# An eight-core transformer layer: transposes moved from TensorE to transposing DMAs, and the start loaded in another order

## The reference, cut to what matters

```python
# x: (8, 4096, 1024) f32, 16 heads of 64, causal
def attn(x):
    q, k, v = split(x @ c_attn_kernel.T + c_attn_bias, 3)      # heads of 64
    s = (q / sqrt(64)) @ k.T + causal_bias
    return (softmax(s) @ v).reshape(b, s, 1024) @ c_proj_kernel.T + c_proj_bias
def ffn(x):
    return gelu(x @ w1 + b1, approximate=False) @ w2 + b2       # 1024 -> 4096 -> 1024
x = _layernorm(x + attn(x))
x = _layernorm(x + ffn(x))
```

## Time and profile before

| | us |
|---|---|
| time before, median of 3 runs | 2211.36 (2210.08 to 2312.66) |
| profiled execution, its own time | 2209.44 |
| its span on the slowest core, core 1 | 2207.9 |
| spans of the eight cores | 2200.8 to 2207.9 |
| TensorE busy on core 1 | 2059.6 |
| ScalarE busy on core 1 | 1328.7 |
| VectorE busy on core 1 | 743.2 |

### The profile page before, as it was taken

One profiled execution on the slowest core, in us unless ns is written; L12 is line 12 of the kernel. 1 busy time (PEld: TensorE's weight loads), 2 busy tenths in 40 slices (PEclk: granted clock), 3 DMA queues, 4 the chain that ended last, 5 costly groups with the idle time before them and its releaser, 6 DMA issues.

```text
span 2207.9 us, 65222 instructions; the slowest of 8 cores (2200.8 to 2207.9 us)
## 1 busy us (share of the span) xinstructions
PE 2059.6 (93%) x30380; PEld 1299.5 (59%) x30380; DVE 743.2 (34%) x1925; ACT 1328.7 (60%) x1602; POOL 219.2 (10%) x182
## 2 busy tenths in 40 slices
PE   7999998989999999997788999999999999999997
PEld 3455565555565556654445666666666666666665
DVE  3543334344343443435121322333223223332321
ACT  1799999999999999998995222222222222222222
POOL 2000000000000000001011221222111112221100
PEclk8999999999999999999899999999999999999999
DMA  9500100021000000002954201111110011111000
GB/s 144 81 12 8 36 8 12 19 34 35 8 13 19 8 24 8 12 10 66 169 88 89 51 27 48 49 49 49 48 48 20 30 48 48 48 48 49 20 20 20
DMA packets 53184, 89.73 MB, mean 41 GB/s; under 512 B 3248, under 2 KB 36656, under 8 KB 51888
## 3 DMA queue, kind: packets, MB, share of 16 engines
q0 software_dynamic: 17184, 33.56, 10.0%
q1 hardware_dynamic: 35728, 52.00, 7.1%
HBM read 93.94 MB, written 25.17 MB: 54 GB/s over the span
## 4 chain that ended last, share of the span: by engine, by line
PE 61%; ACT 29%; DVE 7%; DMA 1%; issue 1%; POOL 0%; POOLq 0%; SPq 0%; DVEq 0%; ACTq 0%
ACT work L610 29%; PE ps L1010 20%; PE ps L1028 19%; PE ps L815 5%; PE ps L452 5%; PE ps L665 4%; PE ps L593 4%; DVE qkv L493 2%; DVE work L621 1%; PE ps L284 1%; PE ps L512 1%; DVE work L690 1%; DMA xT<-xb 1%; DVE stat L517 1%; PE ps L858 1%
## 5 line engine op out<-in xcount | busy, mean ns | idle before, releaser
L610 ACT ACTIVATE work<-ps,cb 128x1024 bf16<-128x1024 f32 (+1 forms) x1088 | 1083.8, 1123 | 66.6 <-PE ps L593 61.6
L1018 ACT ACTIVATE work<-ps,b_s 128x256 bf16<-128x256 f32 x512 | 242.3, 473 | 764.1 <-PE ps L1010 764.1
L665 PEld LDWEIGHTS ps<-qkv,work 64*128 64x128 bf16 x16896 | 434.6, 95 | 292.7 <-PE ps L665 82.7
L665 PE MATMUL ps<-qkv,work 64*128 64x65 bf16 x16896 | 569.8, 193 | 17.9 <-DVE work L690 11.6
L1010 PE MATMUL ps<-work,xT 128*128 128x256 bf16 x4096 | 532.2, 273 | 0.4 <-issue 0.4
L1028 PE MATMUL ps<-qkv,work 128*128 128x512 bf16 x1984 | 509.0, 379 | 0.0
L1010 PEld LDWEIGHTS ps<-work,xT 128*128 128x128 bf16 x4096 | 401.3, 98 | 156.2 <-issue 0.5
L593 PE MATMUL ps<-qkv 64*128 64x512 bf16 x2016 | 366.4, 369 | 65.4 <-ACT work L610 57.8
L1028 PEld LDWEIGHTS ps<-qkv,work 128*128 128x128 bf16 x1984 | 192.9, 98 | 164.1 <-ACT work L1018 0.2
L452 PE MATMUL ps<-xT,work 64*128 64x512 bf16 x896 | 258.3, 377 | 2.9 <-DVE stat L517 1.8
L453 PE MATMUL ps<-xT,work 64*128 64x512 bf16 x896 | 258.4, 377 | 0.0
(11 more groups left out here) (74 smaller groups left out, 1262.2 us busy)
## 6 DMA issues: line engine op xcount, KB each, us to landing
work<-x SPq DMA_DIRECT2D x16, 1024.0 KB, 6.3
out<-work SPq DMA_DIRECT2D x15, 1024.0 KB, 4.1
attn_s<-work SPq DMA_DIRECT2D x64, 128.0 KB, 2.0
xT<-w POOLq DMA_DIRECT2D x8, 1024.0 KB, 14.6
work<-attn_s SPq DMA_DIRECT2D x16, 512.0 KB, 7.7
qkv<-w POOLq DMA_DIRECT2D x16, 512.0 KB, 8.3
xT<-xb POOLq DMA_DIRECT2D x7, 1024.0 KB, 45.4
work<-wqk POOLq DMA_DIRECT2D x7, 512.0 KB, 6.1
```

The source lines that it names most:

```text
L610: lambda: sc.activation(pb, ps, AF.Exp, bias=cb[:, 8 * p + g : 8 * p + g + 1], scale=0.125),
L665: r = t.matmul(bank(6 + h)[:, 65 * c : 65 * c + 65], pbuf[i % NP][rows, pc : pc + 128], w[rows, o : o + 65], start=first and j == 0 and c ...
L1018: lambda: sc.activation(hbuf[ui % 4], bank(4 + ui % 2)[:, 0:TB], AF.Gelu, bias=b1[:, hc : hc + 1]),
```

## The change

1. **Turns by DMA.** A new kind of item, `Lane.turn`, is a transposing DMA from SBUF to SBUF. `turn_block` issues one from SP for a block's `attN` (128x512 into `attC`) as soon as the block is divided, with its store behind it. `norm1` issues one from SP for each half of `x2b` (128x1024 into `x2T`) as soon as it is written. The transposes L704 and L858 and the copies L708 and L865 are gone, and `turn_steps` with them. There are 64 of the first kind and 32 of the second, all in SP's one list.
2. **Start.** `wv[0]` is loaded whole, behind all four quarters of group 0. `first_block` computes the values (`go_v`) in one piece of 32 matmuls behind the scores of unit 0 and the sums of squares. The 40 warming matmuls are 26, and 4 more stand behind each quarter of `x`.
3. **x by blocks.** A group of `xT` is one piece of 4096 columns in each partition (`x_col` gives the column).
4. **The table of exp early.** ScalarE computes `exp` of one constant column at the start.
5. **Values of masked units later.** `behind` puts a unit's values in line 4 units behind it for a block's first unit, 3 for a masked one, 2 for the others. Projections may start 6 units behind a pair's start instead of 3, and the loads of `wp` and `w2` are written one block later.

```diff
+    def turn(self, slot, out, in_, *after):
+        slot.value += 16
+        self.items.append(
+            (lambda e=self.eng: e.dma_start_transpose(out, in_), after, (slot.sem, 16))
         )
         return (slot.sem, slot.value)
...
-        first_x.append(pool.dma(
-            slot(f"x0_{f}"), xTv[:, f : f + 2, 0, :],
-            xb_d[0][:, QB * f : QB * f + 2 * QB].rearrange("p (f c) -> p f c", f=2)))
-        if f % 4 == 0:
-            ld_v0.append(pool.dma(slot(f"wv0_{f}"), wv[0][:, 256 * f : 256 * f + 1024],
-                                  wv_d[0][:, 256 * f : 256 * f + 1024]))
-    ld_qk[0], ld_v[0] = ld_qk0[1], ld_v0[1]
+        first_x.append(pool.dma(slot(f"x0_{f}"), xT[:, QB * f : QB * f + 2 * QB],
+                                xb_d[0][:, QB * f : QB * f + 2 * QB]))
+    ld_qk[0] = ld_qk0[1]
+    ld_v[0] = pool.dma(slot("wv0"), wv[0], wv_d[0])
...
-    warm_done = pe.put(warm, t_warm, t_ones)
+    pe.put(lambda: warm(26), t_warm, t_ones)
+    act.put(lambda: sc.activation(lnst[:, 0:1], cexp[:, 0:1], AF.Exp), t_cexp)
...
+    def x_col(a, fc):
+        return 8 * QB * (a // 4) + QB * fc + 128 * (a % 4)
...
             tok = pe.put(lambda fc=fc: go(fc), first_x[fc // 2], ld_qk0[fc // 4], mark=fc == 7)
-            tok_v = pe.put(lambda fc=fc: go_v(fc), ld_v0[fc // 4], mark=fc == 7)
+            if fc % 2 == 1:
+                warm_done = pe.put(lambda: warm(3 if fc < 7 else 4), t_warm, t_ones)
...
         bound(0, 0)
+        tok_v = pe.put(go_v, ld_v[0])
...
-            turns.append((i, p, g))
+            turn_block(p, g)
...
-        def go():
-            r = a = None
-            for c in range(4):
-                r = t.transpose(pb[:, 128 * c : 128 * c + 128], attN[k % 3][:, 128 * c : 128 * c + 128], idb)
-                a = a or r
-            return a, r
-        attN_free[k % 3] = tok = pe.put(go, done, gb_free[u], ld_idb)
-        gb_free[u] = ev = dve.put(lambda: v.tensor_copy(attC[k % 4], pb[:, 0:512]), tok, attC_free[k % 4])
+        attN_free[k % 3] = tok = sp.turn(
+            slot(f"tn{k % 4}"), attC[k % 4].rearrange("p (c q) -> p c q", c=4), attN[k % 3],
+            uev_tok[0], attC_free[k % 4])
         t_attn[p, g] = attC_free[k % 4] = sp.dma(
-            slot(f"at{k % 4}"), attn_d[:, p, QB * g : QB * g + QB], attC[k % 4], ev)
+            slot(f"at{k % 4}"), attn_d[:, p, QB * g : QB * g + QB], attC[k % 4], tok)
...
+        turn(b, c)
+
+    def turn(b, c):
+        x2b_free[c] = t_xT[b, c] = sp.turn(
+            slot(f"tx{b % 2}_{c}"),
+            x2T[b % 2].rearrange("p (f c) -> p f c", f=8)[:, :, 128 * c : 128 * c + 128],
+            x2b[:, 1024 * c : 1024 * c + 1024], t_x2b[b, c], x2T_free.get(b - 2))
...
-            later.append((need, qk_pairs(p, g) + norm_pair(p, g), start_of[p - 1, 0] + 3 if p > 2 else 0))
+            later.append((need, qk_pairs(p, g) + norm_pair(p, g), start_of[p - 1, 0] + 6 if p > 2 else 0))
...
+    def behind(p, g, j):
+        return 4 if j == 0 else 3 if j >= 4 * g else 2
...
-        while turns and i - turns[0][0] >= 5 and not (gb_open[0] and gb_open[1]) and i >= ready[0]:
-            turn_block(*turns.popleft()[1:])
...
-        hold = 3 if units[waiting[0]][2] == 0 and i + 1 < NU else 2
-        while waiting and i - waiting[0] >= hold:
+        while waiting and (i + 1 == NU or i - waiting[0] >= behind(*units[waiting[0]])):
             queue_values(waiting.popleft())
```

More of the change, by code:

```diff
@@ L50, in dma @@
             (lambda e=self.eng: e.dma_start(out=out, in_=in_), after, (slot.sem, 16))
+        )
+        return (slot.sem, slot.value)
+    def turn(self, slot, out, in_, *after):
+        slot.value += 16
+        self.items.append(
+            (lambda e=self.eng: e.dma_start_transpose(out, in_), after, (slot.sem, 16))
         )
@@ L234, in build_nc, with warm @@
     t_warm = dve.put(lambda: v.memset(sq[0], 0.0))
-    def warm():
+    def warm(n):
         a = None
-        for _ in range(40):
+        for _ in range(n):
             r = t.matmul(bank(6), ones, sq[0], start=True, stop=True)
@@ L403, in go @@
                 o = 1024 * qi + 128 * fc
-                r = t.matmul(bank(4 + qi), wqk[0][:, o : o + 128], xT[:, S * fc : S * fc + QB],
+                r = t.matmul(bank(4 + qi), wqk[0][:, o : o + 128], xT[:, QB * fc : QB * fc + QB],
                              start=fc == 0, stop=fc == 7)
@@ L407, in go, with go_v @@
             return a, r
-        def go_v(fc):
+        def go_v():
             r = a = None
             for n in range(4):
-                r = t.matmul(bank(6 + n // 2)[:, 256 * (n % 2) : 256 * (n % 2) + 256],
-                             xT[:, S * fc + 128 * n : S * fc + 128 * n + 128],
-                             wv[0][:, 256 * fc : 256 * fc + 256],
-                             start=fc == 0 and n % 2 == 0, stop=fc == 7, skip_group_check=True)
-                a = a or r
+                for fc in range(8):
+                    r = t.matmul(bank(6 + n // 2)[:, 256 * (n % 2) : 256 * (n % 2) + 256],
+                                 xT[:, x_col(n, fc) : x_col(n, fc) + 128],
+                                 wv[0][:, 256 * fc : 256 * fc + 256],
+                                 start=fc == 0 and n % 2 == 0, stop=fc == 7, skip_group_check=True)
+                    a = a or r
             return a, r
@@ L480, in go @@
                 o1 = 1024 * qi1 + 128 * fc
[L481 removed]
+                xs = slice(8 * QB * g + QB * fc, 8 * QB * g + QB * fc + QB)
                 tok = two_tiles(
@@ L626, in build_nc @@
     t_p = {}
-    turns = deque()
     attN_free = [None] * 3
@@ L679, in put_half @@
             divide(p, g, t_pv[i])
-            turns.append((i, p, g))
+            turn_block(p, g)
     def divide(p, g, tok):
         n = turn_of[p, g] % 3
-        assert all(turn_of[q, h] % 3 != n for _, q, h in turns)
         acc = PS[:, 3072:4096].rearrange("p (h c) -> p h c", h=2)[:, :, 0:260].rearrange(
@@ L840, in norm1 @@
             lambda: gp.tensor_tensor(y, y, b2b, ALU.add), aff, ld_vec["b2"], pool_last[0])
-    def turn_steps(b, early=False):
-        out = []
-        for c in range(2):
-            def go(c=c):
-                if early:
-                    u = gbank()
-                    pb, held = bank(4 + u).bitcast(BF16), gb_free
-                else:
-                    u = pj_next[0]
-                    pj_next[0] = 1 - u
-                    pb, held = bank(6 + u).bitcast(BF16), pj_free
-                def turns():
-                    r = a = None
-                    for f in range(8):
-                        r = t.transpose(pb[:, 128 * f : 128 * f + 128],
-                                        x2b[:, 1024 * c + 128 * f : 1024 * c + 128 * f + 128], idb)
-                        a = a or r
-                    return a, r
-                tok = pe.put(turns, t_x2b[b, c], held[u], ld_idb)
-                x2b_free[c] = tok
-                held[u] = t_xT[b, c] = dve.put(
-                    lambda: v.tensor_copy(
-                        x2T[b % 2].rearrange("p (f c) -> p f c", f=8)[:, :, 128 * c : 128 * c + 128],
-                        pb.rearrange("p (f c) -> p f c", f=8)),
-                    tok, x2T_free.get(b - 2))
-            out.append((2.0, go))
-        return out
+        turn(b, c)
[4 more added lines that the diff above has]
+            x2b[:, 1024 * c : 1024 * c + 1024], t_x2b[b, c], x2T_free.get(b - 2))
     first_block()
@@ L954, in build_nc @@
                 load_w1()
-            if p == NPAIR - 1 and g == 1:
+            if p == NPAIR - 1 and g == 2:
                 load_w2(0, 8, q2_done[NPAIR - 2])
@@ L985, in build_nc @@
             order[1] = True
-    while turns:
-        turn_block(*turns.popleft()[1:])
     end_pe = t_pv[NU - 1]
@@ L1083, in build_nc @@
             extra.extend(rest if b else proj_steps(b + 1))
-        if hc == 20 and b + 1 < NB:
-            extra.extend(turn_steps(b + 1))
         if hc == 2 and b + 2 < NB:
```

26 lines of the change are left out of this document (8 added, 18 removed).

## The result

| | before | after |
|---|---|---|
| time, median of 4 runs, us | 2210.72 | 2230.06 |
| ratio to before, 95% interval | | 1.0096 (1.0079 to 1.0112) |
| first `exp` begins, median of eight cores | 30.0 | 22.9 |
| from there to the first matmul of the second part | 1151.0 | 1188.2 |
| from there to the end of the span | 1022.6 | 1009.4 |

A forecast was written before the change was run, and what follows sets the result against it. TensorE was taken to bound the second part and nearly all of 25 to 100 us, ScalarE's exp the stretch from 100 to 1184 us. Terms -18.3 - 7 - 3 - 4 + 3 = -29.3 gave a 2182 us median, range 2158 to 2204.

The forecast's parts named there:

- The turns have cover ... at 11 us each they still keep up: Attention: attN is reused after 30 us, so turns one at a time keep up with divisions some 10 us apart.
- landing time T: Time for a transposing DMA to land: 4 us for 128x512, 8 us for 128x1024, bounds 2 to 11 us.
- Edits at nothing: Later values, projection starts at +6 units and moved loads of wp and w2 were to cost nothing.
- -18.3 us in the second part: Second part: 240 transposes of 0.076 us each leave a full TensorE, a gain of 18.3 us.
- The rival of late turns: Second part: 128x1024 turns land later than their 28.5 us cover, about 2256 us; chance 0.05.
- -7 us in the attention: From 100 to 1184 us: freed TensorE time shrinks the 34.2 us of exp waiting by a fifth, later values included.
- -3 us before 100 us: Early attention: 2 us from TensorE's transposes removed, 1 us from VectorE copies and the bank freed; 0 to -5 together.
- -4 us at the start: Start: earlier last quarter of x, new order, better clock and faster first matmuls gain 4 us, range 0 to -8.
- +3 us at the end of the attention: Attention's end: block 1's load_at waits behind the last turn, costing 3 us at a 4 us landing, 10 at 11.
- The rival with the other sign: The slower case: second-part turns of 128x1024 take longer than their cover, about 2256 us; chance 0.05.

The follow-up runs named there:

- g3: f2 with only the six attention turns of blocks 55 to 60, beside the loads of w1 and w2, by TensorE, the rest by DMA: 2186.4 us, ratio 0.9897.
- f4: f2 with all 96 turns by DMA: 2219.8 us, ratio 1.0045.
- e3: Changed kernel with the 64 attention turns replaced by plain, non-transposing DMA copies of the same bytes in 256-byte pieces: 2220.0 us, ratio 1.0048.
- e4: Changed kernel with the values' distance as before (3 units for a block's first unit, 2 for others): 2224.0 us, ratio 1.0068.
- e1: Changed kernel with all 64 attention turns back on TensorE: 2216.8 us, ratio 1.0035.
- e2: Changed kernel with only the last nine attention turns back on TensorE: 2204.4 us, ratio 0.9975.
- g1: f4 with each load of w1 and w2 issued only when the one before has landed: 2219.4 us, ratio 1.0045.
- f1: Changed kernel with the values' distance as before and the last nine attention turns on TensorE: 2197.7 us, ratio 0.9946.
- f2: f1 with block 0's projection steps due 44 units ahead instead of 60: 2188.2 us, ratio 0.9900.
- f3: Kernel before with only the 32 turns of x2b by transposing DMA, all else as before: 2203.8 us, ratio 0.9978.
- g2: f2 with all 64 attention turns by TensorE, only those of x2b by DMA: 2192.4 us, ratio 0.9922.

## Why the prediction failed

Forecast 2182 us, range 2158 to 2204; it came to 2230. With three causes taken out (g3, 2186.4) the kernel is where the forecast was, in part by luck: some terms of the sum were too large and others too small. Of the 43.7 us between the two, 33.4 are the six turns (f4 to g3) and 10.2 the values' distance and the projection's due time together (changed kernel to f4). Against before, g3's eight-core medians are -7.1 us to the first `exp`, -3.5 in A and -14.1 in the second part.

1. **"The turns have cover ... at 11 us each they still keep up"** is the step that failed, by 33 us (f4 to g3). I had measured the cover at 51 to 81 us, where DMA is full, and asked only if the landing time T fits. Even there it was close: the first turn, issued at 47.0 us on core 5, took 28.6 us, and the fourth division waited 2.5 us for it. I did not look at the one other stretch in which POOL loads megabytes, 1000 to 1150 us, nor at divisions there. T was to be 2 to 11 us; the 33 turns issued from 1035 to 1128 us on the eight cores took 13 to 31 us, 23 in the median, and the longest in this stretch followed one another without a pause, so that `attN` and SP were both behind (e3). My bounds came from plain DMAs in long pieces. The program could have warned: a turned block lands in pieces of 128 bf16 (the trace has 512 packets of 256 bytes for one), and the plain store of the same bytes does not (128 packets of 1024).

   And the stops of TensorE without a releaser were in no rival. That the many and long ones come with transposing DMAs beside the loads is shown (18 in the changed kernel, 19 in e4, 20 in f4, up to 14.5 us; none over 3 us in e1, e2, e3, g1 and g3). A few short ones come without any turn in flight: two in each of before, f1 and f2, three in f3, one in g2, up to 6.9 us. That TensorE waits there for its next instructions, which come by q8 through the same 16 engines, fits the stop in the middle of a group, the 16 us of the one packet and the 56 of 67 stops that end just behind such a packet, but was read off the traces, not tried. How the 33 us divide between late turns and stops is open; with plain copies (e3) 10 us of the changed kernel's time were gone.
2. **"Edits at nothing", the later values: wrong by 6 to 7 us** (e4, f1). I had even put them in the gain. The wait of `exp` for scores from 100 to 1000 us did not shrink by a fifth, it grew from 22.0 to 29.6 us in the medians of eight cores; with the old distance it is 24.7. Why a later value makes scores late was not taken apart, nor why it costs three times as much beside turns by TensorE. The +6 starts and the loads of `wp` and `w2` stayed in all experiments but f3, and g3 begins 881 `exp` from 100 to 1000 us, like before: no loss shows, as forecast, though neither was tried by itself.
3. **The removed steps' due time was not seen: 9.5 us** (f1 to f2, where the last turns are by TensorE). `turn_steps` had also been what made the projection of block 0 early. In the changed kernel the seam (start of the last `exp` to the first L985) is 5.3 to 7.5 us, in f2 5.4, in f4 2.9, before 4.0, so there it costs less; f4 stands 4 us below e4, but within both intervals, so what the changed kernel itself loses by it stays open.
4. **-18.3 us in the second part: right in kind, a third too large.** The first addition of one block to that of the next was 63.37 us before and is 62.48 now:
```profile
1282.10 2.48 DVE L1029 TENSOR_TENSOR work<-ps,work 128x512 f32<-128x512 f32 x4 [16.67 <-PE ps L1003]
1344.58 2.48 DVE L1029 TENSOR_TENSOR work<-ps,work 128x512 f32<-128x512 f32 x4 [29.61 <-PE ps L1003]
```
So it is for all 14 such pairs of blocks (medians of eight cores), 12.5 us together. 0.89 us for 16 transposes is 56 ns each, not the 76 of the row of busy time, and 13.4 us for the 240: the sum of busy time is more than what a transpose adds to a full engine. The rival of late turns (T over 28.5 us) did not happen in this part: L985 (L986 in the prediction) waits 0.6 us in 4096 matmuls.
5. **-7 us in the attention: nothing** with the values' distance of before. From 100 to 1000 us not one `exp` was gained by TensorE's freed time (g2, g3). 117 us to spare did not mean that its waits hang on its load. Beside the later values the same turns did take 6.7 us off the wait for scores (e1 to the changed kernel), but the later values had first added 14.4 (g2 to e1). **-3 us before 100 us: right**, 3.4 us (3 `exp` between g2 and g3).
6. **-4 us at the start: 7.** The order came out as forecast, but the clock was not low any more: 1.00 from 20 to 25 us on core 5, before 0.59. The last quarter's matmuls ran without a wait, and the 14 projections took 3.19 us, not 5.38:
```profile
17.64 1.03 PE L412 MATMUL ps<-xT,work 128*128 128x512 bf16 x4
18.50 1.03 PE L242 MATMUL ps<-work,ones 128*128 128x512 bf16 x4
...
21.31 3.67 PE L421 MATMUL ps<-work,xT 128*128 128x256 bf16 x32
...
22.78 1.11 ACT L621 ACTIVATE work<-ps,cb 128x1024 bf16<-128x1024 f32 x1 [20.06 <-DVE cb L342]
...
25.23 3.19 PE L288 MATMUL ps<-xT,work 128*128 128x512 bf16 x14
```
 The last quarter at 17.64 us (forecast 18.2), the first projections at 25.2 (forecast 27 to 31, before 30.1).
7. **+3 us at the end of the attention: right.** `load_at` was issued 3.58 us behind the end of the last division (1212.48 us), before 1.47; L815 waited 2.57 us, before 0.58, and the two groups behind the wait ran longer, 1.75 and 1.91 us instead of 1.03 and 1.04, at a granted clock of 0.66 (1225 to 1230 us; before, behind its wait, 1.00). That is 3.6 us together:
```profile
1216.06 0.55 SPq L50 DMA_DIRECT2D work<-attn_s  x1
...
1225.56 0.61 PE L815 MATMUL ps<-wpT,work 128*128 128x512 bf16 x2 [2.57 <-DMA work<-attn_s]
1226.00 1.75 PE L1003 MATMUL ps<-qkv,work 128*128 128x512 bf16 x4
1227.54 1.91 PE L985 MATMUL ps<-work,xT 128*128 128x256 bf16 x8
```

The rival with the other sign was the right family in the wrong place: late turns, but in the attention, where I had called them covered. Of the page's figure (the Trainium skill, VectorE: DVE Perf Modes, The three transpose paths; 1309 ns for a 128x128 by DMA) the runs say: in a quiet stretch four of them landed together in 2.4 us, less than the 5.2 of four in a row; beside the weight loads ten times that. The rule of the Trainium skill on the same page (VectorE: DVE Perf Modes, Rules for kernel authors), which prefers TensorE for a 128x128 transpose, held for the six turns beside the loads here (33 us, f4 to g3); for the others no run shows a gain by TensorE.

## What to carry to other kernels

Work moved to DMA has to be priced in the busiest stretch of the DMA engines that it will ever meet, by pieces and not by bytes, and a page of the profile's slices shows where that is; leave on the engine the few items that fall there. When a step is taken out of a paced list, look at what else its due time was holding in place. And a bound engine's idle time falls only if its waits came from load: count events by a fixed time (`exp` by 1000 us) in a variant before believing it.

## What the runs showed of the hardware that I had not expected

- A DMA in 256-byte pieces, 128 KB in all, took 2.4 us alone, 9 us beside one casting load (g1) and 13 to 31 us beside two or three in the changed kernel; plain copies in such pieces took 26 and 29 us there (e3). The first turn, beside the loads of `x`, took 28.6 us. The packets of the whole kernel rose from 53184 to 114861 with the change.
- Transposing DMAs beside two or three casting loads came with single packets of all queues that took up to 22.4 us (503 to 521 packets over 3 us in three kernels, at most one in any other), and with stops of TensorE of 3 to 14 us, the longest in the middle of a group of matmuls. The first turn, beside the loads of `x`, came with neither. The granted clock in such a window was 0.64 (g3: 0.98 in the same one) and 0.67 in the next; two matmuls of L604 behind the stop took 0.61 us instead of 0.39.
- Issuing a turn holds SP for 1.2 us, against 0.3 us for a plain store.
- Where the masks on VectorE met an addition on POOL, either one mask took 2.37 us instead of 0.22 and the addition 2.40, or no mask was slowed and the addition took 3.08. Both came with the same starts, the masks 0.3 us ahead (changed kernel, cores 0 to 3 and 4 to 7); what decides is not shown.
